# Weighing one step earlier: PE's products of the step three back now stand ahead of the step's scores

## The reference

```python
# x: 2 x 2048 x 256, H = 16 heads of width 16, values 32 wide
s1 = jnp.einsum('bhqd,bhkd->bhqk', q1, k1) * scale
s2 = jnp.einsum('bhqd,bhkd->bhqk', q2, k2) * scale
a1 = jax.nn.softmax(jnp.where(causal, s1, neg_inf), axis=-1)
a2 = jax.nn.softmax(jnp.where(causal, s2, neg_inf), axis=-1)
comb = a1 - lam[None, :, None, None] * a2
out = jnp.einsum('bhqk,bhkv->bhqv', comb, v)
...
x = _layernorm(x + attention(x))
x = _layernorm(x + feed_forward(x))
```

## Time and profile before

| what | value |
|---|---|
| median of 3 runs | 2097.8 us |
| profiled execution: span from first to last instruction | 2091.4 us |
| around the span (median minus span) | 6.4 us |
| attention, first score product to last turn | about 1082 us (232.0 to 1314.3) |
| PE busy over the span | 1925.5 us, 92% |
| ACT busy over the span | 1468.2 us, 70% |
| ACT exponentials (L811) | 1013.5 us busy, 112.8 us idle before them |
| PE scores (L830) / weighing (L850) | 475.0 us / 611.9 us busy |

### The profile page before, as it was taken

How to read it: one execution, slowest core, us unless ns; L and a number is a source line. 1 busy time by engine, 2 the same in 40 slices (tenths; PEclk the granted TensorE clock), 3 DMA queues, 4 the chain that set the end, 5 groups by cost and what they waited for, 6 DMA issues and landing times. The chain is left out here.

```text
span 2091.4 us, 36204 instructions
## 1 busy us (share of the span) xinstructions
PE 1925.5 (92%) x12400; PEld 1090.7 (52%) x12400; DVE 724.6 (35%) x1543; ACT 1468.2 (70%) x1876; POOL 201.2 (10%) x300
## 2 busy tenths in 40 slices
PE   7994599999899899998999999399999999999997
PEld 5883233333233233332333333278888888888886
DVE  5775021222122221221122212344554535445442
ACT  5663499989899899898998999254444435445452
POOL 0001111111111111111111111000000000000000
PEclk9997699999999999999999999699999999999998
DMA  8997805643366235642564340200101000110000
GB/s 264 361 354 200 134 6 78 83 62 55 51 82 83 36 51 81 83 56 32 79 82 57 52 57 11 81 1 31 31 11 31 22 22 21 33 31 11 11 11 12
DMA packets 137064, 148.83 MB, mean 71 GB/s; under 512 B 76000, under 2 KB 108256, under 8 KB 133760
## 3 DMA queue, kind: packets, MB, share of 16 engines
q1 hardware_dynamic: 134768, 140.55, 33.8%
q10 hardware_dynamic: 1888, 5.24, 1.3%
q0 software_dynamic: 240, 0.66, 0.2%
HBM read 90.85 MB, written 55.57 MB: 70 GB/s over the span
## 5 line engine op out<-in xcount | busy, mean ns | idle before, releaser
L811 ACT ACTIVATE attn_probs<-attn_s_ps 128x1024 f32<-128x1024 f32 (+2 forms) x1152 | 1013.5, 1049 | 112.8 <-PE attn_s_ps L830 106.6
L850 PE MATMUL attn_sums_ps<-attn_probs,heads_v 128*32 128x512 f32 (+3 forms) x5120 | 611.9, 551 | 0.0
L830 PE MATMUL attn_s_ps<-heads_q,heads_k 50*128 50x512 f32 (+3 forms) x2560 | 475.0, 435 | 93.4 <-DMA heads_q<-shift 48.5
L830 PEld LDWEIGHTS attn_s_ps<-heads_q,heads_k 50*128 50x128 f32 x2560 | 218.1, 188 | 577.3 <-ACT attn_probs L811 465.8
L1334 ACT ACTIVATE split_whole<-split_hid_ps,hs 128x512 f32<-128x512 f32 x128 | 88.3, 690 | 274.5 <-PE split_hid_ps L1248 274.3
L895 DVE COPY attn_sums_sb<-attn_sums_ps 128x512 f32<-128x512 f32 x64 | 44.3, 692 | 670.4 <-PE attn_sums_ps L850 666.8
L795 POOL TENSOR_SCALAR_AFFINE_SELECT attn_probs<-attn_probs 128x512 f32<-128x512 f32 x256 | 161.2, 639 | 955.8 <-ACT attn_probs L811 954.6
L1248 PE MATMUL split_hid_ps<-split_hid_b,h2t_r 128*128 128x512 f32 x1024 | 240.6, 392 | 0.0
L1248 PE MATMUL split_hid_ps<-split_hid_a,h1t_r 128*128 128x512 f32 x1024 | 238.1, 391 | 0.0
L1248 PEld LDWEIGHTS split_hid_ps<-split_hid_a,h1t_r 128*128 128x128 f32 x1024 | 190.0, 188 | 41.2 <-DVE split_hid_a L1476 1.4
L1248 PEld LDWEIGHTS split_hid_ps<-split_hid_b,h2t_r 128*128 128x128 f32 x1024 | 189.8, 188 | 38.0
(11 more groups left out here) (123 smaller groups left out, 1567.2 us busy)
## 6 DMA issues: line engine op xcount, KB each, us to landing
qk_parts<-proj_parts SPq DMA_DIRECT2D x64, 512.0 KB, 5.6
heads_q<-qk_parts SPq DMA_DIRECT2D x90, 256.0 KB
heads_k<-qk_parts SPq DMA_DIRECT2D x90, 256.0 KB
proj_w_rows<-in_L_ffn_h_w SPq DMA_DIRECT2D x16, 512.0 KB, 6.5
values<-proj_v SPq DMA_DIRECT2D x8, 1024.0 KB, 6.0
diffs<-attn_diff SPq DMA_DIRECT2D x32, 256.0 KB, 4.5
split_heads<-diffs SPq DMA_DIRECT2D x8, 1024.0 KB, 5.5
heads_v<-values SPq DMA_DIRECT2D x15, 512.0 KB
```

The costliest lines, as they stand in the source:

```text
L811: nc.scalar.activation(weights, side_by_side, ACT.Exp, scale=SCALE).then_inc(exp_done, 1)
L830: last = nc.tensor.matmul(s_ps[n % SLOTS][:, s, place * width:(place + 1) * width], k_sb[u][rows, b * SEQ + j * PARTS:b * SEQ + (j + 1) * ...
L850: last = nc.tensor.matmul(sums[c * D:(c + 1) * D, off:TILE], v_sb[u][:, b * KEY_BLOCKS + j, :], probs[k % PROBS][:, b, s, off:TILE], start ...
```

## The change

Inside a step the two calls change places. At step k PE issues W(k-3), with the turn that belongs to it, and then S(k):

```diff
             def head(h, u, r, first, last):
                 for k in range(NS):
+                    use(h, u, first, k - LAG)
                     for n, (step, _) in enumerate(UNITS):
                         if step == k:
                             scores(h, u, r, first, n)
-                    use(h, u, first, k - LAG)
                 if last:
                     for k in range(NS - LAG, NS):
                         use(h, u, first, k)
```

## The result

| | before | after |
|---|---|---|
| median of 4 runs each | 2097.6 us (2093.9 to 2099.4) | 2111.9 us (2110.6 to 2115.5) |
| profiled span | 2091.4 us | 2112.9 us |

The change makes the kernel slower: the ratio is 1.0076, with a 95% interval of 1.0062 to 1.009. The forecast was 2105.9 us with a range of 2099.5 to 2114. By the ratio the cost is 15.9 us (13.0 to 18.9), where 8.1 were worked out. The two profiled executions lie further apart, 21.5 us, since the one of before was its shortest run and the one of after its longest. So the total is taken from all runs, and the traces are used to tell where it goes.

A forecast was written before the change was run, and what follows sets the result against it. ACT's exponentials were taken to set the pace for most of a head, PE nearly full too. Terms 6.3 + 1.2 + 1.0 - 0.4 = 8.1 us gave 2105.9 us, with an 8 in 10 range of 2099.5 to 2114.

The forecast's parts named there:

- The straight change, +0.7 us nine times: Head changes in straight code: W(0) waits for step 0's mask, so step 4 starts 0.63 to 0.79 us later; 6.3 us.
- The unknown that was bounded: At W(0): the way from POOL's end to a waiting PE, put between nothing and 0.16 us.
- Inside a head, nothing: Away from a head's ends: weighings one step nearer their scores cost 0, at most 0.1 us a head, 1.6 in all.
- The loop edge, +0.2 us six times: At loop jumps: 1.15 us more work up to S(4), less 0.99 as the pause starts earlier; 1.2 us in all.
- The upper case, 1.15 us: At a loop edge: the cost if the pause were tied to something else and did not start earlier.
- The two ends, +0.6 us: Head 0 loses 1.0 us by a weighing ahead of the scores; the end of head 15 gains 0.4.
- The upper end of 1.9 us: Start of head 0: the most one extra weighing ahead of the scores could cost, the slow 1.93 us.
- the 0.4 us: End of head 15: gain from three weighings behind the last scores instead of four, 0.4 counted of 0.99 us.
- The signs that were named: In the profile after: W(0) stands about 0.5 us, edge pauses about 5, head pairs grow 0.9, ACT idle rises some 8.
- A: Rival, last tile of each head: ACT's 0.47 us gap closes and the mask wait goes, 2092.1 us; chance 0.07.
- B: Rival, head changes: exponentials of steps 1 and 2 hide the mask wait at W(0), 2099.6 us; chance 0.13.
- C: Rival, loop edges: pause starts no earlier or slow clock lasts longer, 6.9 and some 3 us, 2114.6 us; chance 0.13.

The follow-up runs named there:

- e4: The changed kernel without the mask of step 0 (POOL doesn't clear that corner, PE doesn't wait for it): 2108.0 us, ratio 1.0053 to the kernel before.
- e9: e8 with tile 0's steps in the order of widths 512, 256, 384, 128, narrow steps apart: 2063.9 us, ratio 0.9848 to the kernel before.
- e10: e7 with tile 0's steps in the order of widths 512, 256, 384, 128: 2054.4 us, ratio 0.9809 to the kernel before.
- e2: The changed kernel with LAG = 4, so before's row with the new call order at the jump: 2095.7 us, ratio 0.9998 to the kernel before.
- e5: The kernel before with 16 increments of an unused semaphore on PE ahead of attention: 2076.2 us, ratio 0.9905 to the kernel before.
- e7: The kernel before with PE's 16 heads written out, no loop on PE: 2050.4 us, ratio 0.9775 to the kernel before.
- e1: The kernel before with LAG = 2, so after's row with the old call order at the jump: 2086.1 us, ratio 0.9949 to the kernel before.
- e6: The changed kernel with 16 increments of an unused semaphore on PE ahead of attention: 2098.9 us, ratio 1.0004 to the kernel before.
- e8: The changed kernel with PE's 16 heads written out, no loop on PE: 2070.0 us, ratio 0.986 to the kernel before.
- e3: The changed kernel with the old order of the two calls at steps 3 to 13 of each head: 2103.6 us, ratio 1.003 to the kernel before.

## Why the prediction was right, and where its terms were off

**The straight change, +0.7 us nine times: right.** The stand at W(0) is 0.51 us from start to start, for 0.45 and up to 0.16 more that were worked out; the lag at step 4 is 0.76 us, inside the 0.63 to 0.79 named. e4 shows the wait for the mask as its cause, and e9 and e10 show that it hangs on the two narrow steps. The unknown that was bounded, the way from POOL's end to PE, is seen in the rows: the mask is 648.44 + 0.64 = 649.08 us, W(0) starts at 649.21. This is POOL in after:

```profile
648.44 0.64 POOL L795 TENSOR_SCALAR_AFFINE_SELECT attn_probs<-attn_probs 128x512 f32<-128x512 f32 x1 [1.36 <-ACT attn_probs L811]
```

It takes 0.13 us, close to the upper end of that bound.

**Inside a head, nothing: wrong.** Each head but the first loses another 0.20 us at step 12, 3.0 us over fifteen heads, nearly twice the upper bound of 1.6. The step that failed is the claim behind the 0, that a shifted row costs only where W stands and waits. By the rows, shifting by one step also changes *which width* stands between a point at which ACT holds PE and the next place where ACT needs scores. PE in before, from S(10) on:

```profile
650.01 0.73 PE L830 MATMUL attn_s_ps<-heads_q,heads_k 50*128 50x512 f32 x4
650.67 0.85 PE L850 MATMUL attn_sums_ps<-attn_probs,heads_v 128*32 128x384 f32 x8
651.45 0.44 PE L830 MATMUL attn_s_ps<-heads_q,heads_k 50*128 50x128 f32 x4
651.82 1.07 PE L850 MATMUL attn_sums_ps<-attn_probs,heads_v 128*32 128x512 f32 x8
652.82 0.73 PE L830 MATMUL attn_s_ps<-heads_q,heads_k 50*128 50x512 f32 x4
```

The same stretch in after, from W(7) on:

```profile
660.13 0.85 PE L850 MATMUL attn_sums_ps<-attn_probs,heads_v 128*32 128x384 f32 x8
660.92 0.95 PE L830 MATMUL attn_s_ps<-heads_q,heads_k 50*128 50x512 f32 x4
661.79 1.06 PE L850 MATMUL attn_sums_ps<-attn_probs,heads_v 128*32 128x512 f32 x8
662.79 0.44 PE L830 MATMUL attn_s_ps<-heads_q,heads_k 50*128 50x128 f32 x4
663.16 1.07 PE L850 MATMUL attn_sums_ps<-attn_probs,heads_v 128*32 128x512 f32 x8
664.15 0.73 PE L830 MATMUL attn_s_ps<-heads_q,heads_k 50*128 50x512 f32 x4
```

The weighing of width 384, W(7), stood behind S(10) and stands ahead of it. The 0.2 us that it is shorter are now spent waiting for ACT inside S(10), which takes 0.87 us from start to start instead of 0.66. Behind S(10) two full weighings lie ahead of S(12), where it was one full and one of 384: 661.79 to 664.15 is 2.36 us, 650.67 to 652.82 is 2.15. ACT is short of scores at step 12 and the difference of 0.21 us goes into the end of the head. The expectations of the experiments still put these 0.2 us down to a wait for the mask of step 10; the rows show about 0.1 us of such a stand, and it isn't what sets S(12). No run changes the width of W(7) alone, so this reading is argued from the rows and not shown by a run.

**The loop edge, +0.2 us six times: right in sign, wrong in its working.** The upper case, 1.15 us, was the nearer one. The step that failed is that the pause starts 0.99 us earlier because W(35) is gone from in front of it. Up to S(4) the traces differ by 0.92 us where the slow clock lasts equally long. The pause is not tied to the groups in the row but to the jump, and PE's sequencer reaches the jump 0.6 us after the group behind the last held scores has started: in before W(35) at 697.41 and the jump at 698.04, in after W(36) at 708.75 and the jump at 709.33. The first product then comes 7.40 us after 697.41 in before (S(0), 704.81) and 7.30 us after 708.75 in after (W(37), 716.05). The groups that PE still has queued (1.36 us of work before, 0.37 after) run beside the pause and change nothing. So nothing is saved, and W(37) is in front of S(0) at the slow clock. ACT's gap at an edge grows from 5.2 to 6.0 us to 7.2 to 7.5 us.

From the first exponential behind one edge to that behind the next, two heads take 135.7 to 136.3 us in before. In after they take 138.2 to 138.5 us three times and 141.4 us twice. Less the 0.97 and the 0.20 us that the two heads lose in the row, an edge costs 0.9 to 1.3 us, and 3.9 and 4.6 us in the two long pairs; all six come to about 10.7 us in these two traces. In the long pairs one thing can be seen: in after's trace the 1.2 GHz level holds for 6.8 us at most edges and for 17.1 us at two of six (570.8 to 587.8 and 850.6 to 867.7). Windows of 20 us around edges of after (granted clock before the last two figures; the first and third are the long ones), with the earlier trace rows as the counterpart:

```profile
563.00:583.00 20.00, 13.90 (x82) 4.00 (x82) 0.69 (x1) 10.50 (x13) 3.12 (x5) 0.69 0.01 2
704.00:724.00 20.00, 14.05 (x100) 4.15 (x96) 0.69 (x1) 11.37 (x14) 3.08 (x5) 0.83 0.01 2
843.00:863.00 20.00, 13.88 (x82) 3.86 (x82) 0.69 (x1) 10.28 (x12) 3.12 (x5) 0.69 0.01 2
```

The heads behind the long stretches took 69.0 us, where 65.3 to 65.8 is usual in after. Before's trace has five edges with 6.8 us and one with 10.2. Why the level holds longer there isn't shown by any run.

**The two ends, +0.6 us: not settled at the start, nothing gained at the end.** The first head is 2.2 us longer in after's trace, not 1.0. The timeline shows why the estimate was low: W(0) waits in front of S(3) for its exponential, and runs at 1.2 GHz. PE in after, at the start of head 0:

```profile
234.57 1.94 PE L850 MATMUL attn_sums_ps<-attn_probs,heads_v 128*32 128x512 f32 x8 [1.08 <-ACT attn_probs L811]
```

The upper end of 1.9 us had been the slow weighing alone. But the first head differs as much between runs of one row: with the row of before it takes 65.2 to 68.7 us (before, e2, e5, e7), with that of after 66.5 to 70.0 (after, e1, e6, e8). From e5 to e6 it grows by 1.25 us and from e7 to e8 by 4.3, so no run fixes this term.

At the end of head 15 the 0.4 us were a gain that didn't come. The last turn starts 2.55 us behind the end of the last exponential in before (1311.05 to 1313.60) and 2.54 us in after (1332.65 to 1335.19). There are three weighings behind the last scores instead of four, but the last of them waits for its mask. PE in after:

```profile
1333.11 1.28 PE L850 MATMUL attn_sums_ps<-attn_probs,heads_v 128*32 128x512 f32 x16 [0.78 <-POOL attn_probs L795]
```

**The sum.** Straight changes 9 x 0.76 = 6.8 for 6.3; step 12, 15 x 0.20 = 3.0 for 0; the end 0 for -0.4. What is left of the 15.9 us is 6.1 (3.2 to 9.1) for the edges and the first head together, for which 1.2 + 1.0 were worked out; it is a remainder and not measured by itself, and the runs' times don't part the two. So of the 7.8 us that the sum was short, 3.0 lie inside the head, 3.9 at the edges and the start, 0.5 at the straight changes and 0.4 at the end. That the time still fell into the range, 2 us below its upper end, owes something to luck: the range had room for a costlier edge, and the cost inside the head, for which 1.6 us at most had been kept, fitted into the same room.

**The signs that were named.** The stands at W(0), the later start of step 4, the pause at the edges and the unchanged stages behind attention came as written. ACT's idle total rose by 22.6 us, where 8 were named. Each pair of heads from edge to edge was to grow by 0.9 us, and a growth of over 2 us was named as the sign of a cost inside the head or at the edge that had been put at nothing. The pairs grew by 2.1 to 2.4 us, and by 5.1 and 5.7 us where the slow level held long. By its own sign, then, the prediction was wrong in these two terms, and the runs found both.

**The rivals.** A is refuted: the gap of 0.37 us in the last tile is unchanged in every head, since the sum of the groups ahead of it is. B is refuted by ACT's 1.01 us. C's time (2114.6) is nearer to the result than the forecast, and its first half, that the pause starts no earlier, is true; its 6.9 us for six edges fit the 0.9 to 1.3 us of the usual ones in the traces. Its whole, 6.9 and 3 for the clock, is more than the 6.1 us that the runs leave for the edges and the first head together, and the 3.0 us inside the head were not in it.

## What to carry to other kernels

When an order is shifted by a step, read the row of widths between each point where the pacing engine holds the other and the next place where it is short, not only the new waits: a group that gets shorter in front of a held point gains nothing, and the longer one behind it costs in full. At a jump the pause counts from the jump and not from the work queued before it, so put scores, or whatever the pacing engine waits for, first behind it. And before tuning what stands at a jump, write the loop out or move its body by a few instructions: here that was worth 46 and 20 us, more than the order of the work.

## What the runs showed of the hardware

- A taken branch of PE's sequencer lasts 3.3 to 3.9 us. The first product comes 3.5 to 4.2 us after its start if the body begins at number 3 of a block of 256 instructions (e1, e5, e6), but 6.4 to 7.3 us if it begins at number 243 (before, after, e3, e4). 16 instructions of padding moved the time of the kernel by 1% (20.6 us).
- The length of a pause alone doesn't tell what the clock does. Behind such pauses PE's products mostly run at 1.2 GHz for a while (a weighing 1.93 instead of 1.06 us): for 6.8 us at most edges, at two of after's for 17.1. In e5 two edges with the same pause of 1.87 us differ: behind one the clock stayed at 2.4 GHz, behind the other it was at 1.2 GHz for 6.8 us.
- A wait of the weight loads is not a wait of PE: in e4 they waited for POOL for 20.2 us, PE's products for 1.5.
- From the end of a POOL instruction to the waiting product it takes 0.13 us.
